# Four units routed ahead in the memory stage, the routing reordered, and expert tiles of 128 rows

## The chip, the cores and the metric

One core of a Trainium2 chip runs the whole program; the other cores are idle. The metric is the device time of one execution in microseconds (us). The core's engines are PE (TensorE: matmuls and transposes), DVE (VectorE), ACT (ScalarE), POOL (GpSimd) and SP (SyncE, which here only issues DMAs). Each has its own instruction queue; they meet through semaphores.

## The reference

The input x is 4 x 1024 tokens of 128 numbers, fp32. Four residual layers follow each other:

```python
x = x + attn(layernorm(x))     # softmax attention and a causal linear "memory" term, 16 heads
x = x + ffn(layernorm(x))
x = x + mamba(layernorm(x))    # selective scan, 256 inner channels, state 16
x = x + ffn(layernorm(x))

def ffn(x):                    # x: 4096 tokens x 128
    shared = (silu(x @ sw1) * (x @ sw2)) @ sw3           # 128 -> 256 -> 128
    probs = softmax(x @ rw + rb)                         # 8 experts
    w, idx = top_k(probs, 2); w = w / sum(w)
    routed = sum over the two chosen e of  w_e * ((silu(x @ ew1[e]) * (x @ ew2[e])) @ ew3[e])
    return shared + routed
```

The reference computes every expert for every token; the kernel computes for each token only the two chosen ones.

## The kernel before

**Stages in time.** Projection (0 to 87 us of the profiled span), softmax attention (to 618), the memory term (to 752), the first FFN's routing (to 841) and its experts (to 968), the scan (to 1545), the second FFN's routing (to 1641) and experts (to 1768), and a last sum of the rows.

**The memory stage** (`memory`, L934 on) walks over 32 blocks t of 128 tokens, eight for each of four batches. For each block PE makes masked products, which DVE masks in three parts and POOL in the fourth; then outputs, then a state of 128x128 that goes on to the next block. Four blocks are a half, which is also a unit of 512 tokens: when a half is done it is projected, x is added (`add_x`) and the result x1 is stored to DRAM by ACT (`store_x1`, two alternating tiles and semaphores). SP loads each batch ahead (`load_batch`). Into this loop the routing of the first two units of the next FFN is woven by hand, at given blocks: DVE's `mean_dve` (statistics of the layer norm), POOL's `rstd_pool`, DVE's `norm_dve`, PE's `turn_pe` (transposes), `logits_pe`, DVE's `choose_dve` and `settle_dve` (top 2), ACT's `tanh_act` (the gates), PE's `rank_pe` (ranks of the tokens within their experts by matmuls with a triangle), DVE's `place_dve` and `label_dve` (rows and token numbers), and POOL's `scatter`. These PE steps share the PSUM tile ps_p with `turn_ka` and `project_half`, so the waits of these are set by the order of the steps. SP loads the units' x back from DRAM at L1123 to L1129, after the third batch's load and the router's weights rw and rb (`load_choice`, L1409 and L1410).

**The routing** (`Router`, L1360 on, and `route`, L1576 on). A unit of 512 tokens gives 1024 pairs of token and expert; a scatter is an indirect DMA issued by POOL that writes 128 normalized rows, each with its token number and gate, to the row of `ex` in DRAM that its expert and rank give: eight scatters a unit, 64 for 4096 tokens. In `route`, `first` is the number of units that were routed ahead (2 in the first FFN, 0 in the second). The last of these is held: its eight scatters are issued in `route`. Each turn s also runs one unit of the shared FFN: `share_pe` and `silu_act`, `share_dve`, `back_pe` (L1628), `base_dve`, and a store by SP. When the last unit is placed, DVE makes two small tables: for each expert tile its expert (`name_experts`, L1831 to L1844) and its first row of `ex` (`name_rows`, L1853 to L1858), by wide operations over tiles x 8. Zero rows are stored behind each expert's rows (`pads`) so that a last tile reads valid rows.

**The experts** (`run_experts`, L1861 on). Each expert's rows are cut into tiles of ROWS = SUB x 128; with whole tiles per expert there are at most TOP * N / ROWS + 8. A loop runs over AHEAD tiles, unrolled, and jumps back. For each tile: SP reads the first row from the table into a register and loads the rows (AHEAD buffers); DVE reads the expert's number and copies the two weight matrices ew1 and ew2 to a fixed tile (L1933); PE transposes the rows (L1977), ACT evicts xT (L2007), PE makes ps_h (L1970), ACT the silu (L2002), DVE the product hid (L1940), PE makes ps_o (L1959) with ew3 at an address from a register that it loads at L1953, ACT evicts with the gate (L1995), POOL scatters 128 rows of results to `ey` (L2021). PE works on three tiles in one turn of its body, in this order:

```python
e = pe.value_load(at_expert[0:1, number_of(ti, tq)])   # L1953: tile q - 3
pe.wait_ge(hid_ready, now(s - 2))
...                                                    # ps_o, SUB x 2 matmuls, L1959
pe.wait_ge(xT_ready, now(s + 0))                       # tile q - 1
pe.wait_ge(w12_ready, now(s + 0))                      # L1967
...                                                    # ps_h, 4 matmuls, L1970
pe.wait_ge(loaded[q], now(i * 16 + 16))                # tile q
pe.wait_ge(xT_ready, now(s - 1))                       # L1975
...                                                    # SUB transposes, L1977
```

## Time and profile before

| | us |
|---|---|
| runs of the kernel before | 1784.13, 1785.74, 1794.47 |
| their median | 1785.74 |
| the profiled execution's own time | 1792.23 |
| its span, first to last instruction | 1790.5 |
| mean granted clock of PE | 0.859 |
| busy over the span: PE, DVE, POOL, ACT | 1362.6, 1266.3, 880.4, 855.2 |

The profile is of one execution. PE is the matmul array, PEld its weight loads (which overlap), PEq or PEldq the queue that reads PE's instructions; a share of busy time over the whole span is a mean over stages with different limits, so the stages are read one by one. A fp32 matmul stands in the rows as two instructions, a transpose as one. Matmuls are pipelined: the row's duration of one reaches into the next, and the distance of two starts is what one costs. The idle time before an instruction stands in brackets with what ended it ("issue" where nothing that the profile shows did).

### The profile page before, as it was taken

The page shows a single profiled execution, that of the slowest core. Times are in us where ns is not written, and L with a number is a line of the kernel's source. Part 1 is how long each engine was busy: PE and PEld are TensorE (multiplying, and loading weights), DVE is VectorE, ACT ScalarE, POOL GpSimd, SP SyncE. Part 2 cuts the span into 40 slices and gives each one's busy share as a digit, 9 for nine tenths or more (in the row PEclk, how much of TensorE's full clock was granted, in tenths as well). Part 3 has the DMA queues.
Part 4 walks back from the last instruction along what each step waited for, and adds up shares of the span by engine and source line. Part 5 has one row for each costly group of instructions (what it writes and reads, how often), then busy time and mean ns, then how long its engine had stood idle before and what let it go on. Part 6 is the DMA issues. An engine that isn't in the chain of part 4 may idle for free. (4 is left out here: it accounts for less than half of the span.)

```text
span 1790.5 us, 27815 instructions
## 1 busy us (share of the span) xinstructions
PE 1362.6 (76%) x8207; PEld 677.6 (38%) x8208; DVE 1266.3 (71%) x2981; ACT 855.2 (48%) x1215; POOL 880.4 (49%) x775
## 2 busy tenths in 40 slices
PE   3448999999999898785995777586676544584993
PEld 1213333333333265553994232131221200353992
DVE  3666899999989267674333279998998999573343
ACT  3403666666666734221553668467476332121551
POOL 3400212121211454675665248869869666475662
PEclk9655999999999999997997888698788656797996
DMA  4821111111112232254333395976957863624336
GB/s 121 265 73 48 53 49 55 47 58 44 61 47 65 54 84 84 86 159 108 85 93 111 98 226 154 249 182 162 245 131 199 198 163 94 174 87 124 111 93 166
DMA packets 218312, 210.68 MB, mean 118 GB/s; under 512 B 49247, under 2 KB 188482, under 8 KB 215874
## 3 DMA queue, kind: packets, MB, share of 16 engines
q1 hardware_dynamic: 196174, 180.70, 37.7%
q0 software_dynamic: 9216, 19.02, 3.3%
q10 hardware_dynamic: 12800, 9.46, 1.8%
q8 instruction: 60, 0.98, 0.2%
q14 instruction: 62, 0.51, 0.1%
HBM read 145.27 MB, written 63.37 MB: 117 GB/s over the span
## 5 line engine op out<-in xcount | busy, mean ns | idle before, releaser
L804 ACT ACTIVATE attn_prob<-attn_ps_cols 128x1024 f32<-128x1024 f32 (+1 forms) x320 | 292.0, 940 | 219.7 <-PE attn_ps_cols L680 218.7
L2546 POOL TENSOR_TENSOR ssm_hc<-ssm_h,ssm_cb 128x1024 f32<-128x1024 f32 x128 | 300.5, 2355 | 136.1 <-DVE ssm_h L2529 112.3
L2529 DVE TENSOR_TENSOR_SCAN ssm_h<-ssm_decay,ssm_ps_u 128x1024 f32<-128x1024 f32 x128 | 292.7, 2287 | 29.9 <-ACT ssm_decay L2517 12.6
L830 POOL TENSOR_SCALAR_AFFINE_SELECT attn_prob<-attn_prob 128x512 f32<-128x512 f32 x128 | 81.2, 635 | 415.7 <-ACT attn_prob L804 415.7
L712 DVE CUSTOM_DVE_ANT_0 attn_ps_rows<-attn_ps_rows,const_mask_rows 128x384 f32<-128x384 f32 (+3 forms) x512 | 236.1, 522 | 39.5 <-PE attn_ps_rows L647 37.3
L647 PE MATMUL attn_ps_rows<-attn_ks,attn_qs 72*128 72x512 bf16 (+3 forms) x768 | 228.8, 351 | 44.3 <-DMA attn_qs<-parts_dram 31.0
L2517 ACT ACTIVATE ssm_decay<-ssm_wide,ssm_aneg 128x1024 f32<-128x1024 f32 x128 | 146.1, 1146 | 173.5 <-DVE ssm_h L2529 97.1
L2480 PE MATMUL ssm_ps_u<-ssm_stack,ssm_spread 96*128 96x512 bf16 x256 | 99.1, 479 | 154.0 <-DVE ssm_h L2529 147.4
L680 PE MATMUL attn_ps_cols<-attn_qs,attn_ks 75*128 75x512 bf16 (+3 forms) x768 | 194.3, 333 | 4.6 <-DMA attn_qs<-attn_nrows 3.9
L699 PE MATMUL attn_ps_o<-attn_prob,attn_vw 128*32 128x512 f32 (+3 forms) x1536 | 166.6, 506 | 0.3 <-POOL attn_prob L830 0.3
L717 DVE TENSOR_REDUCE attn_nm<-attn_ps_rows 128x1 f32<-128x512 f32 x256 | 157.8, 682 | 7.8 <-PE attn_ps_rows L647 7.7
L2524 DVE TENSOR_TENSOR ssm_ps_u<-ssm_ps_u,ssm_bb 128x1024 f32<-128x1024 f32 x128 | 154.8, 1209 | 8.7 <-PE ssm_ps_u L2480 8.7
L647 PEld LDWEIGHTS attn_ps_rows<-attn_ks,attn_qs 72*128 72x128 bf16 x768 | 71.4, 100 | 180.4 <-DVE attn_nm L712 65.0
L2480 PEld LDWEIGHTS ssm_ps_u<-ssm_stack,ssm_spread 96*128 96x128 bf16 x256 | 17.3, 103 | 252.9 <-DVE ssm_h L2529 202.7
L680 PEld LDWEIGHTS attn_ps_cols<-attn_qs,attn_ks 75*128 75x128 bf16 x768 | 69.9, 100 | 87.8 <-ACT attn_prob L804 35.5
L2021 POOL DMA_INDIRECT ey_dram<-ffn1e_out,ffn1e_x x80 | 76.6, 957 | 50.9 <-ACT ffn1e_out L1995 38.3
L2021 POOL DMA_INDIRECT ey_dram<-ffn2e_out,ffn2e_x x80 | 76.6, 957 | 50.1 <-ACT ffn2e_out L1995 37.5
L2496 PE MATMUL ssm_ps_y<-ssm_hc,ssm_gather 128*32 128x512 f32 x512 | 83.4, 782 | 7.6 <-POOL ssm_hc L2546 7.6
L1970 PE MATMUL ffn1e_ps_h<-ffn1e_xT,ffn1e_w 128*128 128x256 f32 x320 | 77.6, 386 | 0.9 <-ACT ffn1e_xT L2007 0.9
L1970 PE MATMUL ffn2e_ps_h<-ffn2e_xT,ffn2e_w 128*128 128x256 f32 x320 | 77.1, 384 | 0.9 <-ACT ffn2e_xT L2007 0.9
L1096 DVE TENSOR_TENSOR mem_am<-mem_ps_a,const_strict 128x512 f32<-128x512 f32 x96 | 60.3, 684 | 20.6 <-PE mem_ps_a L1014 20.5
L1940 DVE TENSOR_TENSOR ffn1e_hid<-ffn1e_act,ffn1e_ps_h 128x512 f32<-128x512 f32 x40 | 27.5, 688 | 66.0 <-PE ffn1e_ps_h L1970 66.0
(361 smaller groups left out, 2438.6 us busy)
## 6 DMA issues: line engine op xcount, KB each, us to landing
ssm_wide<-delta_dram SPq DMA_DIRECT2D x128, 512.0 KB, 6.4
attn_ks<-parts_dram SPq DMA_DIRECT2D x48, 192.0 KB
attn_qs<-parts_dram SPq DMA_DIRECT2D x48, 192.0 KB
parts_dram<-proj_parts SPq DMA_DIRECT2D x8, 768.0 KB, 3.8
ffn1e_x<-ex_dram SPq DMA_DIRECT2D x40, 130.0 KB, 2.3
ffn2e_x<-ex_dram SPq DMA_DIRECT2D x40, 130.0 KB, 2.3
split_dram<-ssm_parts SPq DMA_DIRECT2D x6, 768.0 KB, 4.3
ssm_stack<-split_dram SPq DMA_DIRECT2D x18, 256.0 KB, 4.5
```

Of the source, the lines that this page charges most:

```text
L647: done = nc.tensor.matmul(out[:, x * w:(x + 1) * w], qs[k][0:KROWS, h, blk * P:(blk + 1) * P], ks[k][0:KROWS, h, half * QW:half * QW + w], ...
L680: done = nc.tensor.matmul(out[:, x, 0:w], ks[k][:, h, j * P:(j + 1) * P], qs[k][:, h, at:at + w], start=True, stop=True, skip_group_check= ...
L699: done = nc.tensor.matmul(ps_o[32 * h:32 * h + 32, at - ch * QW:at - ch * QW + w], vw[k % 2][:, j, h, :], prob[u % RING][:, h, 0:w], start ...
L712: done = nc.vector.tensor_tensor_reduce(scores, scores, c["mask_rows"][:, QW - w:], -1.0, -MINUS, ALU.add, ALU.min, into[:, h, at:at + 1])
L717: nc.vector.tensor_reduce(to, ps_rows[bank][:, 0:len(heads) * w].rearrange("p (h w) -> p h w", w=w), AX.X, ALU.max, negate=True).then_inc( ...
L804: nc.scalar.activation(prob[u % RING][:, heads[0]:heads[-1] + 1, 0:w], ps_cols[s % 2][:].rearrange("p b (x q) -> p (b x) q", x=len(heads) ...
L1970: done = nc.tensor.matmul(ps_h[n][z][:, h, :], w12[z][:, n * HIDDEN + h * P:n * HIDDEN + (h + 1) * P], xT[z][:], start=True, stop=True)
L2021: nc.gpsimd.indirect_dma_start(dram["ey"], bass.IndirectOffsetOnAxis(ap=x[q][:, j, TOKEN:TOKEN + 1].bitcast(I32), axis=0), out[q % OUTS][: ...
L2517: nc.scalar.activation(decay[t % DECAY_RING][:], wide[t % WIDE_RING][:], ACT.Exp, scale=aneg[:, at:at + 1]).then_inc(decay_ready, 1)
L2524: nc.vector.tensor_tensor(ps_u[t % 2][:], ps_u[t % 2][:], bb[b % 2][:], ALU.mult).then_inc(dbx_done, 1)
L2529: nc.vector.tensor_tensor_scan(h[t % H_RING][:], decay[t % DECAY_RING][:], ps_u[t % 2][:], 0.0, ALU.mult, ALU.add).then_inc(scan_done, 1)
L2546: nc.gpsimd.tensor_tensor(hc[:, t % HC_RING, :], h[t % H_RING][:], cb[b % 2][:], ALU.mult).then_inc(hc_done, 1)
```

## The change

- **Memory stage.** Four units instead of two are routed ahead, on one regular plan: unit u has its statistics at block 9 + 4u, norm and rstd at 10 + 4u, transposes at 11 + 4u, logits and choice at 12 + 4u, settle at 13 + 4u, the gates at 14 + 4u, rank, place and label at 15 + 4u. `set_up_dve` goes from block 9 to 8. From block 16 to 27 POOL issues two scatters per block (24, units 0 to 2; before, 8 in blocks 24 to 27). x1 is stored one block earlier. SP loads units 0 and 1 back after the third batch's load, units 2 and 3 after the fourth's.
- **Routing.** `first` is 4 in the first FFN: 8 held scatters and 32, where it was 8 and 48. While units 4 to 6 are routed, two units of the shared FFN run per turn. Within a turn the shared part stands between the logits and the rank; in the turn of the last unit the table of experts is made before the shared part, and the table of rows after it. xT has a tile for each unit.
- **Experts.** Tiles of 128 rows: 72 where it was 40, twelve in a turn of the loop where it was eight, six output tiles where it was eight. The zero rows are half as many.

```diff
@@ memory
-TURNED_BEHIND = {5: 1, 7: 2}
+STATS_AT, NORM_AT, TURN_AT, LOGITS_AT, SETTLE_AT, TANH_AT, RANK_AT, SEND_AT = 9, 10, 11, 12, 13, 14, 15, 16
+def unit_at(t, first):
+    u, rest = divmod(t - first, HALF)
+    return u if rest == 0 and 0 <= u < AHEAD_UNITS else None
@@ memory: sync
                         load_choice(sp, r, a)
-                        for u in range(AHEAD_UNITS):
-                            sp.wait_ge(x1_stored[u], 16)
+                    if i >= 2:
+                        for u in (2 * i - 4, 2 * i - 3):
+                            sp.wait_ge(x1_stored[u % 2], u // 2 * 16 + 16)
...
@@ memory: vector
-                    if t == 9:
+                    if t == 8:
                         set_up_dve(nc, r, c, dve)
-                    if t in (12, 15):
-                        mean_dve(nc, r, dve, (t - 12) // 3)
-                    if t in (13, 16):
-                        norm_dve(nc, r, dve, (t - 13) // 3)
+                    if unit_at(t, STATS_AT) is not None:
+                        mean_dve(nc, r, dve, unit_at(t, STATS_AT))
+                    if unit_at(t, NORM_AT) is not None:
+                        norm_dve(nc, r, dve, unit_at(t, NORM_AT))
...
@@ memory: scalar
-                    if t % HALF == 0 and half >= 2:
-                        store_x1(half - 2)
+                    if t % HALF == HALF - 1 and half >= 1:
+                        store_x1(half - 1)
@@ memory: gpsimd
-                    if t in (12, 15):
-                        rstd_pool(nc, r, pool, (t - 12) // 3)
-                    if 24 <= t < 28:
+                    if unit_at(t, NORM_AT) is not None:
+                        rstd_pool(nc, r, pool, unit_at(t, NORM_AT))
+                    if SEND_AT <= t < SEND_AT + (AHEAD_UNITS - 1) * HALF:
                         for j in range(2):
-                            scatter(nc, r, dram, pool, 0, (t - 24) * 2 + j)
+                            scatter(nc, r, dram, pool, (t - SEND_AT) // HALF, (t - SEND_AT) % HALF * 2 + j)
@@ sizes
-SUB = 2
+SUB = 1
-AHEAD = 8
-OUTS = 8
+AHEAD = 12
+OUTS = 6
+SENT = 4
-AHEAD_UNITS, AHEAD_ENDS = 2, [1, 2, 3, 5, 7, UNITS_IN]
-EXPERT_STRIDES = [AHEAD, 16, SUB * 16]
+AHEAD_UNITS, AHEAD_ENDS = 4, [1, 2, 3, 4, 5, 7, UNITS_IN]
+EXPERT_STRIDES = [AHEAD, 16]
@@ route
+        def shared_in(s):
+            if not first:
+                return [s - 1] if s else []
+            done = 2 * (s - first)
+            return [u for u in (done, done + 1) if u < s] if s < UNITS_IN - 1 else [s - 1]
@@ route: tensor
-                for u in range(first - 1):
-                    share_pe(u, 0)
-                    share_pe(u, 1)
-                for s in range(first, UNITS_IN + 2):
+                for s in range(first, UNITS_IN + 1):
+                    shares = shared_in(s)
                     if s < UNITS_IN:
                         turn_pe(nc, r, c, s)
-                    if s >= 2:
-                        back_pe(s - 2)
+                    if shares:
+                        pe.wait_ge(s_loaded, 3 * 16)
+                        share_pe(shares[0], 0)
                     if s < UNITS_IN:
                         logits_pe(nc, r, s)
-                    if 1 <= s <= UNITS_IN:
-                        share_pe(s - 1, 0)
-                        share_pe(s - 1, 1)
+                    if shares:
+                        if shares[0]:
+                            back_pe(shares[0] - 1)
+                        share_pe(shares[0], 1)
                     if s < UNITS_IN:
                         rank_pe(nc, r, s)
+                    if len(shares) > 1:
+                        share_pe(shares[1], 0)
+                        back_pe(shares[0])
+                        share_pe(shares[1], 1)
+                back_pe(UNITS_IN - 1)
@@ route: vector (the order within a turn)
+                    if s < UNITS_IN:
+                        choose_dve(nc, r, dve, s)
+                        settle_dve(nc, r, dve, s)
+                    if s + 1 < UNITS_IN:
+                        norm_dve(nc, r, dve, s + 1)
+                    if shares:
+                        share_dve(dve, shares[0], 0)
+                        if shares[0]:
+                            base_dve(dve, shares[0] - 1)
+                        share_dve(dve, shares[0], 1)
+                    if s < UNITS_IN:
+                        place_dve(nc, r, dve, s)
+                        label_dve(nc, r, dve, s)
+                    if s == UNITS_IN - 1:
...
                         steps = name_experts(nc, dve, t, r.count, step_dve, tabled)
...
+                name_rows(nc, dve, t, step_dve, tabled, steps)
+                base_dve(dve, UNITS_IN - 1)
```

## Rows read from the trace of the kernel before

**Rows 1.** Busy time by stretch: engine, busy us (instructions); then PE clock, DMA share, GB/s.

```profile
618.00:752.40 134.40, 121.49 (x1587) 79.10 (x1587) 89.28 (x219) 47.70 (x83) 73.28 (x70) 0.94 0.30 84
752.40:841.00 88.60, 58.69 (x294) 38.72 (x294) 53.81 (x283) 18.35 (x35) 65.11 (x66) 0.85 0.53 149
841.00:968.00 127.00, 116.86 (x720) 104.97 (x720) 44.71 (x81) 64.19 (x160) 77.02 (x82) 0.96 0.31 84
...
1641.00:1768.00 127.00, 116.32 (x720) 104.67 (x720) 45.07 (x80) 64.19 (x160) 76.58 (x80) 0.96 0.36 101
```

**Rows 2.** Timeline of PE, experts, first FFN: start, us, line, operation, tiles, count.

```profile
868.99 1.89 PE L1970 MATMUL ffn1e_ps_h<-ffn1e_xT,ffn1e_w 128*128 128x256 f32 x8
870.72 0.38 PE L1977 MATMUL ffn1e_ps_x<-const_ident,ffn1e_x 128*128 128x128 f32 x2
870.94 1.06 PE L1959 MATMUL ffn1e_ps_o<-ffn_w,ffn1e_hid 128*128 x8
871.83 1.89 PE L1970 MATMUL ffn1e_ps_h<-ffn1e_xT,ffn1e_w 128*128 128x256 f32 x8
```

**Rows 3.** PE's queue in one tile: line, operation, ns min/median/max, first and last start.

```profile
L1953 PEldq TENSOR_LOAD <-ffn_at_expert x2: 303/304/305, 866.3 to 869.1; - x2
L1959 PEldq SEQ_ASSERT  x4: 18/18/18, 867.0 to 867.7; - x4
L1967 PEldq EVENT_SEMAPHORE  x1: 51/51/51, 867.9 to 867.9; - x1
L1975 PEldq EVENT_SEMAPHORE  x1: 51/51/51, 868.8 to 868.8; - x1
```

**Rows 4.** Timeline of ACT, the same tile: the eviction of xT.

```profile
868.38 0.39 ACT L2007 ACTIVATE ffn1e_xT<-ffn1e_ps_x 128x256 f32<-128x256 f32 x1 [0.56 <-PE ffn1e_ps_x L1977]
```

**Rows 5.** PE's queue, last two loads of an expert number in the loop's end.

```profile
L1953 PEldq TENSOR_LOAD <-ffn_at_expert x2: 301/302/303, 956.8 to 958.4; - x2
```

**Rows 6.** Groups by line and shape, experts: busy us, mean ns | idle before.

```profile
L2021 POOL DMA_INDIRECT ey_dram<-ffn1e_out,ffn1e_x x80 | 76.6, 957 | 50.9 <-ACT ffn1e_out L1995 38.3 <-issue 12.3 <-DMA ey_dram<-ffn1e_out,ffn1e_x 0.3
L1933 DVE COPY ffn1e_w<-ffn_w 128x512 f32 x40 | 17.1, 429 | 21.1 <-issue 19.0
```

**Rows 7.** Timeline of SP's DMA issues, memory stage.

```profile
655.84 0.35 SPq L979 DMA_DIRECT2D early_qaT<-fT_dram  x1
...
661.64 2.19 SPq L1409 DMA_DIRECT2D ahead_rw<-in_L_ffn_rw_dram  x1
...
664.48 10.35 SPq L1127 DMA_DIRECT2D ahead_x<-x_dram  x2
```

**Rows 8.** The tile ahead_x in 655 to 680 us: from DMA issue to landing.

```profile
DMA to landing us min/median/max: 2.8/3.7/4.6
```

**Rows 9.** Timeline of DVE, memory stage: the end of set_up_dve.

```profile
662.65 0.17 DVE L1573 TENSOR_SCALAR ahead_count<-ahead_number 128x8 f32<-128x8 f32 x1
```

**Rows 10.** Waits in 630 to 750 us: engine, line, releaser: us in total, times, longest.

```profile
PE mem_ps_y L1037 <- POOL mem_am L1285: 4.4, 2, 2.3
```

**Rows 11.** Timeline of POOL, memory stage: the mask around two scatters.

```profile
727.19 1.28 POOL L1285 TENSOR_TENSOR mem_am<-mem_raw,const_strict 128x512 f32<-128x512 f32 x1
...
730.93 1.27 POOL L1285 TENSOR_TENSOR mem_am<-mem_raw,const_strict 128x512 f32<-128x512 f32 x1
```

**Rows 12.** Timeline of POOL, first routing: its last scatter.

```profile
837.36 0.95 POOL L1549 DMA_INDIRECT ex_dram<-ffn1r_xn,ffn1r_pos  x1 [0.31 <-issue]
```

**Rows 13.** Timeline of PE, first routing: one unit to the next.

```profile
801.72 2.05 PE L1628 MATMUL ffn1r_ps_o<-ffn1r_sw,ffn1r_hid 128*128 128x128 f32 x16 [0.24 <-DVE ffn1r_hid L1608]
...
804.42 3.68 PE L1621 MATMUL ffn1r_ps_h<-ahead_xnT,ffn1r_sw 128*128 128x512 f32 x8
...
808.93 2.05 PE L1628 MATMUL ffn1r_ps_o<-ffn1r_sw,ffn1r_hid 128*128 128x128 f32 x16 [0.23 <-DVE ffn1r_hid L1608]
```

**Rows 14.** Timeline of DVE, first routing: one wide operation on the tables.

```profile
819.93 0.48 DVE L1840 TENSOR_TENSOR ffn_mine<-ffn_begun,ffn_over 1x320 f32<-1x320 f32 x1
```

**Rows 15.** Timeline of POOL, second routing: its first scatter.

```profile
1553.61 1.11 POOL L1549 DMA_INDIRECT ex_dram<-ffn2r_xn,ffn2r_pos  x1 [4.51 <-DVE ffn2r_xn L1436]
```

More of the change, by code:

```diff
@@ L1137, in _ @@
                         products(t + 1)
+                    u = unit_at(t, RANK_AT)
+                    if u is not None:
+                        if u == 0:
+                            pe.wait_ge(r.set_up, 3)
+                        pe.wait_ge(x1_ready, u + 3)
+                        rank_pe(nc, r, u)
                     outputs(t)
@@ L1730, in _ @@
-                    if first < s < UNITS_IN:
-                        choose_dve(nc, r, dve, s)
-                        settle_dve(nc, r, dve, s)
-                    if s == first + 2:
-                        for u in range(first + 5, UNITS_IN):
+                    if len(shares) > 1:
+                        share_dve(dve, shares[1], 0)
+                        base_dve(dve, shares[0])
+                        share_dve(dve, shares[1], 1)
+                    if s <= first + 1:
+                        for u in range(first + 3 + 2 * (s - first), min(first + 5 + 3 * (s - first), UNITS_IN)):
@@ L1735, in _ @@
                             mean_dve(nc, r, dve, u)
[L1736 to L1738 removed]
+                name_rows(nc, dve, t, step_dve, tabled, steps)
+                base_dve(dve, UNITS_IN - 1)
             @block.scalar
             def _(act):
[L1742 to L1744 removed]
                 for s in range(first, UNITS_IN + 1):
+                    shares = shared_in(s)
@@ L2013, in _ @@
                 m.wipe(pool)
-                turns = Turns(pool, stage + "_pool", sorted(set(EXPERT_STRIDES + [SUB * AHEAD])), first=1)
+                turns = Turns(pool, stage + "_pool", EXPERT_STRIDES, first=1)
                 def body(i, at, q, on):
@@ L2083, in routing_scratch @@
     for stage in stages:
-        dram[stage + "r_sent"] = [m.sem(f"{stage}_sent{k}") for k in range(DEEP)]
+        dram[stage + "r_sent"] = [m.sem(f"{stage}_sent{k}") for k in range(SENT)]
         dram[stage + "e_sent"] = [m.sem(f"{stage}_out{q}") for q in range(AHEAD)]
```

137 lines of the change are left out of this document (49 added, 88 removed).

## The prediction

> **What bounds the kernel now.** I read the busy time by stretch first, because the change touches four stretches with different limits [rows 1]. In each expert stage PE is busy 116.9 of 127 us, and no other engine is near it. In the memory stage PE is busy 121.5 of 134.4 us. In the first routing no engine is full: POOL leads with 65.1 of 88.6 us. Attention and the scan keep their code, so they keep their time.
>
> Next I read PE's timeline in the expert stage. One 256-row tile repeats every 2.84 us (868.99 to 871.83) [rows 2]. The spacing of starts prices it: eight ps_h instructions from 868.99 to 870.72, 0.216 each; two transposes, 0.22; eight ps_o instructions from 870.94, 0.89, so 0.111 each. The array is never idle, so today it sets the pace.
>
> Third came PE's queue, the part that reads instructions and fills registers. It loads the expert's number (L1953) at 866.3 and at 869.1, works out the weight addresses, and reaches the wait of L1967 at 867.9 [rows 3]. That is 1.6 us of scalar work per tile, whatever the tile's height. Then it stands until 868.8 (L1975). ACT's eviction of xT runs from 868.38 for 0.39 us, to 868.77 [rows 4]: the queue goes on when xT is there. So the 0.9 us from L1967 to L1975 is mostly waiting, and the 1.6 us is work, hidden today under 2.84 us of array. At the stage's end, with no new tile to transpose, two loads still stand 1.6 us apart (956.8, 958.4) [rows 5].
>
> **The change, part 1: experts, 72 tiles of 128 rows.** Array work per tile: ps_h 8 x 0.111, one transpose 0.11, ps_o 4 x 0.111, together 1.44 us. 72 x 1.44 = 103.7 against 40 x 2.84 = 113.6: on the array alone, less. The queue's work per tile shrinks only by the steps of the second half, two of the four assertions of L1959 (four lie between 867.0 and 867.7) [rows 3], about 0.2. What remains is 1.6 - 0.2 = 1.4 from load to L1967; from L1975 to the next load 0.3 (868.8 to 869.1); and the wait's own 0.05 plus the reading of eight ps_h instructions, which the rows do not separate from the waiting. I take 0.15 for both, because the queue reads the ps_o instructions within its 1.6 as well. Sum 1.85, and with the jump back once in twelve tiles about 1.9 us. The chain transpose, xT, ps_h of one tile does not exceed it: 0.89 of the ps_h ahead in the array, 0.27 for the transpose, 0.39 at most for the eviction, 1.55. Nor do others: POOL's scatter takes 0.957 and a pause of 0.30, 1.26 a tile; DVE copies weights for 0.43 as before, since a tile's weights don't shrink [rows 6].
>
> Bounds for this period: below, 1.44, if the array hides all the queue's work; above, 1.4 + 0.3 + 0.9 = 2.6, if nothing between L1967 and L1975 is waiting. I take 1.9, nearer the lower end, because the queue resumed within 0.1 us of the eviction's end.
>
> Per FFN: 127.0 today is 113.6 and 13.4 of fill and drain. The drain is three tiles deep, so it shortens by 3 x (2.84 - p). After: 72p + 13.4 - 3 x (2.84 - p) = 75p + 4.9. Against 127.0 that is 75p - 122.1; at p = 1.9, +20.4. Both FFNs: **+41**. At the bounds -28 and +146.
>
> This rests on the scalar load's 0.303 us [rows 3]. The Trainium skill ("DMA: Bandwidth & Descriptors", Latency and other measured facts) gives a floor of about 600 ns for a `tensor_load`, and says that the compiler unrolls fourfold to amortize it, a rule against small tiles. This trace shows half that price; by the page's, an estimate of p = 2.2 and of +86 for this term.
>
> **Part 2: memory stage.** DVE's statistics for unit 0 move to block 9, behind set_up_dve, which ends at 662.8 [rows 9]. The x they need is loaded by SP behind the batch load that starts at 655.84 and behind rw and rb; it is issued at 664.48 [rows 7] and lands up to 4.6 later [rows 8]: 669.1. DVE would stand 6.3 us, and its products' masks and state, for which PE waits, are queued behind. Unit 2, at block 17, meets the same order behind the next batch load without rw and rb (2.8 us less): I take 4.5. Removed: PE's waits on POOL's mask, which stands behind rstd, 4.4 us in two waits [rows 10]. Added on PE: turn, logits and rank of two more units, each 7.21 - 5.4 = 1.8 (part 3), +3.6. Added on POOL: 16 scatters; a block with two of them takes POOL 3.74 us (727.19 to 730.93) [rows 11], against a block of 134.4 / 32 = 4.2, so POOL is close to the pace in twelve blocks instead of four: 0 to 8, I take 4. Where one stall covers another I take off 2. Sum 6.3 + 4.5 - 4.4 + 3.6 + 4 - 2 = **+12**, bounds +2 (x is in time) and +18.
>
> **Part 3: first routing.** Sixteen scatters fewer. The last one starts at 837.36, and one costs 0.95 + 0.31 = 1.26 [rows 12]: POOL's chain shortens by 20.2. PE becomes the tighter one for a while. A unit takes 7.21 us on PE (801.72 to 808.93); the shared FFN's part is 3.5 of L1621 and 1.9 of L1628, 5.4, the durations less the overlap with what follows [rows 13]. Two shares per routed unit make 10.8 + 1.8 = 12.6, over 8 x 1.26 = 10.1 of POOL. So the gain is not whole: three such rounds lose 2.5 each over POOL's pace, but the first begins before POOL's scatters of its unit, and I count about 3 lost. Behind them the tables: a wide operation takes 0.48 us on 320 elements [rows 14]; on 576 I scale it to 0.75. Eight of them, +2.2, and they now stand ahead of the last unit's share and sum, which must still run and be stored. 20.2 - 3 - 2.2 = **-15**; bounds -21 and -12. The halved zeros and the longer tables that POOL writes among its scatters I set against each other.
>
> **Part 4: second routing.** All 64 scatters stay, one behind another from 1553.61 on; the first waits 4.51 us for unit 0 [rows 15]. The new order lets unit 0 be placed without norm of later units ahead of it: **-1**, bounds -3 and +2.
>
> **Sum.** 41 + 12 - 15 - 1 = +37 on the profiled execution: its own time is 1792.23 (span 1790.5), which is 6.5 over the median 1785.74 of the runs. I add the difference to the median: 1785.7 + 37 = 1823, stated as 1822.
>
> **The rivals.** (B, the other side) The queue's work is hidden: the array holds enough instructions that the scalar work of one tile runs under the matmuls of another, and the chain of 1.55 us sets p = 1.55 or less. For it: the array is never idle today [rows 2]. Against it: the queue stands at L1967 until xT is there [rows 3, 4], so it can't run ahead into the next tile. At p = 1.5, 75 x 1.5 - 122.1 = -9.6 for each FFN; -19 + 12 - 15 - 1 = -23, so 1763. It decides from p below 1.655, where the whole sum is nought; a time under 1768 needs p = 1.54. The Trainium skill ("Advanced Engine Details and Errata", Sequencer Loop) says that other engine instructions can be read and queued while a control instruction executes. If that held across tiles, p would be 1.5; the rows that show the queue released by xT speak against it.
>
> (C) x is not late in the memory stage, because x1 is stored one block earlier and SP is there in time. Against it: SP, not the store, was late (rw, rb and the batch load ahead) [rows 7]. Then +2 for that stage: 41 + 2 - 15 - 1 = +27, 1813.
>
> (D) PE's clock falls in the expert stages. PE would stand idle 0.46 of each 1.9 us, where today it never stands [rows 2]; the granted clock is 0.96 in the expert stage, and 0.85 in the first routing, where PE stands between its units [rows 1]. If a sixth of the tiles ran at the lower level, 1.2 instead of 2.4 GHz, they would take 2 x 1.44 = 2.88: 24 tiles x 0.98 = +24, so 1846.
>
> (E) In between: p between 1.54 and 1.77, since the reading of ps_h may cost nothing and the address work may be shorter in other code. Then the time lies from 1768 to 1803, no change that counts.
>
> **How the numbers follow.** Forecast (p near 1.9, x late) 0.43, D 0.17, C 0.11, E 0.19, B 0.10. A measurement of this kernel can tell about 1%, 18 us, from no change: faster is under 1768, slower over 1803.6. Faster 0.10 (B), same 0.19 (E), slower 0.71. The range 1790 to 1850 takes in the forecast, C, D and the upper half of E; below it lie B and E's lower half, above it a period nearer 2.6, a price that only the upper bound has.
>
> **What would show it right or wrong.** In the expert stage of after: distance of successive TENSOR_LOADs of PE's queue about 1.9 us, PE busy about 105 of 147 us, and L1967's wait at once followed by L1975, no 0.9 us between. If the loads stand 1.5 apart, part 1 is wrong and the kernel may be faster. In the memory stage: SP's load of the first x issued after DVE's set_up, statistics idle about 6 us on a DMA, the stage near 146 us. In the first routing: 40 scatters, end of stage 73 us after its start. The granted clock of the expert stage tells D. Most of all the forecast falls if the queue's 1.6 us is not work but pace kept by something behind it.

## The result

The changed kernel took 1828.5 us (median of 4 runs, 1826.2 to 1830.5) against 1785.5 for the kernel before: 1.021 times, with a 95% interval of 1.0185 to 1.0234. It is slower by 43 us, 2.1%, with an interval clear of no change and on both sides of 2%; 1822 was forecast, with 1790 to 1850 as the range.

The busy time by stretch of the changed kernel (us; PE, PEld, DVE, ACT, POOL, each with its instructions; then granted clock, DMA share, GB/s):

```profile
618.30:772.00 153.70, 128.61 (x1621) 83.45 (x1621) 108.29 (x299) 50.56 (x89) 91.60 (x88) 0.91 0.30 84
772.00:845.50 73.50, 53.70 (x260) 35.26 (x260) 46.79 (x204) 15.82 (x29) 47.48 (x49) 0.88 0.49 143
845.50:987.30 141.80, 133.00 (x936) 114.31 (x936) 69.63 (x144) 74.14 (x216) 69.04 (x72) 0.97 0.25 68
...
1660.60:1804.80 144.20, 133.43 (x936) 114.63 (x936) 68.63 (x144) 74.14 (x216) 68.91 (x72) 0.96 0.30 81
```

From the first instruction of each stage to the first of the next, in the two profiled executions:

| stage | before | after | difference | forecast |
|---|---|---|---|---|
| up to the memory stage | 618.7 | 618.9 | +0.2 | 0 |
| memory | 133.8 | 153.1 | +19.3 | +12 |
| first routing | 88.6 | 73.5 | -15.1 | -15 |
| first experts | 126.4 | 141.8 | +15.4 | +20.4 |
| scan | 568.6 | 568.4 | -0.2 | 0 |
| second routing | 104.7 | 104.9 | +0.2 | -1 |
| second experts | 125.9 | 144.2 | +18.3 | +20.4 |
| join | 23.7 | 23.9 | +0.2 | 0 |

So the routing gave back what it was meant to give, and the two expert stages and the memory stage took 53 us.

**The experts.** PE's timeline in the first expert stage of the changed kernel:

```profile
880.64 1.06 PE L1975 MATMUL ffn1e_ps_h<-ffn1e_xT,ffn1e_w 128*128 128x128 f32 x8
881.53 0.27 PE L1982 MATMUL ffn1e_ps_x<-const_ident,ffn1e_x 128*128 128x128 f32 x1
881.66 0.94 PE L1964 MATMUL ffn1e_ps_o<-ffn_w,ffn1e_hid 128*128 x4
882.44 1.06 PE L1975 MATMUL ffn1e_ps_h<-ffn1e_xT,ffn1e_w 128*128 128x128 f32 x8
```

A tile repeats every 1.80 us (880.64 to 882.44), where 2.84 stood for twice the rows [rows 2]. The four ps_o instructions last from 881.66 to 882.44, 0.78, though they need 4 x 0.111: the array stands within them. PE's queue in the same stretch (line, operation, ns min/median/max, first and last start):

```profile
L1958 PEldq TENSOR_LOAD <-ffn_at_expert x2: 300/304/307, 880.8 to 882.6; - x2
L1972 PEldq EVENT_SEMAPHORE  x3: 51/51/51, 880.4 to 884.1; - x3
L1980 PEldq EVENT_SEMAPHORE  x3: 51/51/51, 880.6 to 884.3; - x3
```

The load still takes 0.30. The queue reaches the wait for the weights (L1972; before, L1967) at 880.4 and goes through the next one (L1980; before, L1975) at 880.6. Before, 0.9 us stood between those two [rows 3]; now nothing waits there. In 62 of the stage's 64 tiles that have both events in the trace, 0.25 us or less lie between them. The queue is not released late: it is itself late.

The second expert stage grew by 3 us more than the first. Only there SP loads `ffn_base` behind the first twelve tiles' rows (L1923, 12.0 us from issue to landing), and the rows of the next tile are issued behind it; PE stands for them:

```profile
1673.38 0.82 SPq L1923 DMA_DIRECT2D ffn_base<-base_dram  x1
1685.69 0.32 PE L1982 MATMUL ffn2e_ps_x<-const_ident,ffn2e_x 128*128 128x128 f32 x1 [1.11 <-DMA ffn2e_x<-ex_dram]
```

Around it two tiles took 4.02 and 2.78 us instead of 1.80. That the load of `ffn_base` makes these rows late is read from the order of the queue; no run takes it away.

**The memory stage.** Its waits in the changed kernel (engine, line, releaser: us in total, times, longest):

```profile
DVE ahead_stats L1419 <- DMA ahead_x<-x_dram: 7.8, 2, 6.2
PE mem_ps_p L1493 <- DVE ahead_count L1472: 7.6, 2, 4.2
...
PE mem_ps_y L1043 <- POOL mem_am L1285: 2.3, 3, 1.1
```

DVE stood 7.8 us on the x that SP loads back, 6.2 of it for unit 0, whose load stands in SP's queue behind a batch load and the router's weights. The wait of PE on POOL's mask fell from 4.4 [rows 10] to 2.3. PE has a wait that was not there: the transposes of a unit stand behind the counts of the unit before (L1493), 7.6 us in two waits. DVE's norm in its timeline, with POOL's beside it:

```profile
672.71 1.11 DVE L1434 TENSOR_SCALAR ahead_xn<-ahead_x,ahead_mv,ahead_rstd 128x128 f32<-128x128 f32 x4
...
690.20 3.29 DVE L1434 TENSOR_SCALAR ahead_xn<-ahead_x,ahead_mv,ahead_rstd 128x128 f32<-128x128 f32 x4
...
730.49 4.84 DVE L1434 TENSOR_SCALAR ahead_xn<-ahead_x,ahead_mv,ahead_rstd 128x128 f32<-128x128 f32 x4
```

```profile
689.30 2.35 POOL L1278 TENSOR_TENSOR mem_xb<-early_x,mem_bias 128x1024 f32<-128x1024 f32 x1
691.61 1.28 POOL L1285 TENSOR_TENSOR mem_am<-mem_raw,const_strict 128x512 f32<-128x512 f32 x1
...
730.89 1.27 POOL L1285 TENSOR_TENSOR mem_am<-mem_raw,const_strict 128x512 f32<-128x512 f32 x1
732.12 2.35 POOL L1278 TENSOR_TENSOR mem_xb<-mem_x_in,mem_bias 128x1024 f32<-128x1024 f32 x1
```

Four norm instructions take 1.11 us at 672.71, but 3.29 and 4.84 at 690.20 and 730.49, where POOL adds the bias to x (L1278) and masks (L1285); those at 709.98 take 2.55, beside a scatter and a mask. The last group ends at 735.33, 0.9 us after POOL's addition; its first instruction alone took 4.07 us. The groups by line of the changed kernel (us in all, mean ns; the norm of the memory stage), and the same of the kernel before:

```profile
L1434 DVE TENSOR_SCALAR ahead_xn<-ahead_x,ahead_mv,ahead_rstd 128x128 f32<-128x128 f32 x16 | 11.8, 797 | 0.0
```

```profile
L1436 DVE TENSOR_SCALAR ahead_xn<-ahead_x,ahead_mv,ahead_rstd 128x128 f32<-128x128 f32 x8 | 2.2, 341 | 0.0
```

An instruction that took 341 ns takes 797 in the mean. Counted over all of DVE's operations of the stage, as time beyond the shortest of the same kind (where it is over 0.06 us), this standing is 10.4 us in the changed kernel, in seven instructions, each beside POOL's mask or addition. In the kernel before it is 1.2 us in three; the largest stood beside the mask of [rows 11], where one of two instructions took 0.83 us and the other 0.15:

```profile
727.67 0.91 DVE L1455 TENSOR_TENSOR ahead_gap<-ahead_top 128x4 f32<-128x4 f32 x2
```

**The first routing.** POOL and PE of the changed kernel, and a wide operation of the table of experts:

```profile
819.06 0.95 POOL L1544 DMA_INDIRECT ex_dram<-ffn1r_xn,ffn1r_pos  x1 [2.39 <-DVE ffn1r_xn L1486]
...
840.22 0.96 POOL L1544 DMA_INDIRECT ex_dram<-ffn1r_xn,ffn1r_pos  x1 [0.30 <-issue]
```

```profile
809.02 0.60 PE L1493 MATMUL ffn1r_ps_x<-const_ident,ffn1r_xn 128*128 128x128 f32 x4
...
821.30 0.60 PE L1493 MATMUL ffn1r_ps_x<-const_ident,ffn1r_xn 128*128 128x128 f32 x4
```

```profile
832.88 0.74 DVE L1845 TENSOR_TENSOR ffn_mine<-ffn_begun,ffn_over 1x576 f32<-1x576 f32 x1
```

A round of two shared units and one routed unit takes PE 12.28 us (809.02 to 821.30), POOL waits for the place of the next unit (2.39 at 819.06), and the last scatter ends at 841.2, 69 us after the stage began; before, it ended 86 us after [rows 12].

### The profile page after: what moved, and what is told of

Read it like the earlier page. It is cut to its first block and busy times, and to the rows that moved or that the text cites. A ratio compares the mean times of both kernels' runs of the same rounds, so it can differ in the third digit from the quotient of the medians.

```text
span 1828.7 us, 30675 instructions
## 1 busy us (share of the span) xinstructions
PE 1395.8 (76%) x8639; PEld 697.1 (38%) x8640; DVE 1327.5 (73%) x3110; ACT 875.7 (48%) x1327; POOL 867.3 (47%) x760
## 5 line engine op out<-in xcount | busy, mean ns | idle before, releaser
L2529 DVE TENSOR_TENSOR ssm_ps_u<-ssm_ps_u,ssm_bb 128x1024 f32<-128x1024 f32 x128 | 154.9, 1210 | 10.3 <-PE ssm_ps_u L2485 10.2
L647 PEld LDWEIGHTS attn_ps_rows<-attn_ks,attn_qs 72*128 72x128 bf16 x768 | 71.5, 100 | 180.6 <-DVE attn_nm L712 64.9
L2026 POOL DMA_INDIRECT ey_dram<-ffn2e_out,ffn2e_x x72 | 68.9, 957 | 76.1 <-ACT ffn2e_out L2000 72.0
L2026 POOL DMA_INDIRECT ey_dram<-ffn1e_out,ffn1e_x x72 | 69.0, 959 | 75.3 <-ACT ffn1e_out L2000 72.5
L1975 PE MATMUL ffn2e_ps_h<-ffn2e_xT,ffn2e_w 128*128 128x128 f32 x576 | 79.1, 282 | 0.7 <-ACT ffn2e_xT L2012 0.7
L1975 PE MATMUL ffn1e_ps_h<-ffn1e_xT,ffn1e_w 128*128 128x128 f32 x576 | 78.7, 281 | 0.7 <-ACT ffn1e_xT L2012 0.7
L1938 DVE COPY ffn2e_w<-ffn_w 128x512 f32 x72 | 38.3, 532 | 55.8 <-issue 32.5
L1544 POOL DMA_INDIRECT ex_dram<-ffn2r_xn,ffn2r_pos x64 | 62.6, 979 | 23.4 <-issue 17.7
```

Of the source, the lines that this page charges most:

```text
L647: done = nc.tensor.matmul(out[:, x * w:(x + 1) * w], qs[k][0:KROWS, h, blk * P:(blk + 1) * P], ks[k][0:KROWS, h, half * QW:half * QW + w], ...
L1975: done = nc.tensor.matmul(ps_h[n][z][:, h, :], w12[z][:, n * HIDDEN + h * P:n * HIDDEN + (h + 1) * P], xT[z][:], start=True, stop=True)
L2026: nc.gpsimd.indirect_dma_start(dram["ey"], bass.IndirectOffsetOnAxis(ap=x[q][:, j, TOKEN:TOKEN + 1].bitcast(I32), axis=0), out[q % OUTS][: ...
L2529: nc.vector.tensor_tensor(ps_u[t % 2][:], ps_u[t % 2][:], bb[b % 2][:], ALU.mult).then_inc(dbx_done, 1)
```

## The experiments

Stages of every run, from its own trace (us; the tile is the middle value of the distance between the ps_h of successive tiles in the first expert stage). Runs given below without a ratio are single executions. The kernel before had medians of 1789 to 1794 us beside the experiments and 1785.5 beside the changed kernel, so single runs are compared by their stages rather than by the whole time:

| run | memory | routing 1 | experts 1 | routing 2 | experts 2 | tile |
|---|---|---|---|---|---|---|
| before | 133.8 | 88.6 | 126.4 | 104.7 | 125.9 | 2.84 |
| changed | 153.1 | 73.5 | 141.8 | 104.9 | 144.2 | 1.80 |
| t128_only | 133.6 | 88.7 | 141.0 | 104.9 | 142.2 | 1.80 |
| t256_rest | 153.0 | 74.9 | 126.7 | 104.8 | 126.1 | 2.84 |
| fixed_w3 | 153.1 | 73.4 | 128.6 | 104.7 | 128.5 | 1.63 |
| two_loads | 154.1 | 71.3 | 141.3 | 104.7 | 142.0 | 1.80 |
| turned_first | 153.4 | 73.4 | 140.9 | 104.8 | 143.3 | 1.81 |
| turned_first_fixed_w3 | 152.8 | 73.4 | 116.4 | 105.1 | 122.2 | 1.45 |
| two_loads_used | 153.0 | 73.4 | 169.5 | 105.1 | 168.7 | 2.24 |
| x_direct | 146.3 | 73.4 | 141.8 | 105.4 | 142.3 | 1.80 |
| bias_later | 159.2 | 73.0 | 141.0 | 105.1 | 142.1 | 1.80 |
| both_256 | 147.1 | 75.1 | 126.2 | 104.8 | 127.2 | 2.84 |
| all_128 | 147.6 | 71.5 | 116.1 | 105.2 | 122.6 | 1.45 |
| all_128_bias1 | 146.7 | 71.9 | 115.8 | 105.0 | 120.2 | 1.45 |

**Which half of the change costs what.** The tiles alone in the kernel before:

```diff
-SUB = 2
+SUB = 1
-AHEAD = 8
-OUTS = 8
+AHEAD = 12
+OUTS = 6
```

> The kernel before with only the expert tiles changed (72 of 128 rows, 12 in a turn, 6 output tiles; the scatters of the routing count on four semaphores instead of eight, as in the changed kernel, which leaves semaphores for the 12). Theory A (PE's queue sets 1.84 us per tile): the two expert stages grow as in the changed kernel, by 15 and 18 us, and the wider tables add 0 to 4 us, so 1820 us (1814 to 1826). Rival (the expert stages are slow only behind the new routing, or most of the 43 us comes from the memory stage): at most half of that, under 1805.

Measured: 1823.6 us, 1.0165 of the kernel before (1.0126 to 1.0203), about 30 us. The expert stages grew by 14.6 and 16.3, the routing by 0.1: theory A, and the wider tables add at most 0.2 us to a routing.

The other half, tiles of 256 rows back in the changed kernel:

```diff
-SUB = 1
+SUB = 2
-AHEAD = 12
-OUTS = 6
+AHEAD = 8
+OUTS = 8
```

> The changed kernel with 40 expert tiles of 256 rows again; memory stage and routing stay as changed. Theory A: what is left is the memory stage (+19 us) and the first routing (-15), and the narrower tables give back up to 2 us each: 1788 us (1783 to 1794), its expert stages at 2.84 us per tile again. Rival (the two parts need each other, for instance because the routing's gain comes from the smaller tiles and their fewer zero rows): the first routing longer than 80 us, or the total over 1797.

Measured: 1799.0 us beside 1792.4 for the kernel before in the same runs, 1.0032 (1.0013 to 1.0051). The time itself lies above the expected range and above the rival's 1797. But both were reckoned from a kernel before of 1785.5: the difference expected was -2.5 to +8.5 us, and 6.5 was measured; the routing is far from the rival's 80 us.

The expert stage is as before, the routing keeps 13.7 us of its gain, and the memory stage keeps its 19. The two ratios multiply to 1.0197, close to the whole change's 1.021: the halves do not need each other.

**Is it PE's queue?** PE reads no number; all tiles take the third weights of expert 0:

```diff
-                        e = pe.value_load(at_expert[0:1, number_of(ti, tq)])
...
-                                flat[:, ds(e + (2 * HIDDEN + h * D), D)],
+                                flat[:, 2 * HIDDEN + h * D:2 * HIDDEN + (h + 1) * D],
```

> The changed kernel, in which PE doesn't read the expert's number: ps_o is made with the third weights of expert 0 for every tile, so the routed part of the result is that of another network; all else, the copies of the first two weights too, is as it was. Theory A (the scalar work of PE's queue sets the pace): the distance of two tiles falls from 1.80 us to the next bound, the chain transpose, xT, ps_h of 1.55 us or the array's 1.44, so 144 tiles give back 36 to 52 us: 1777 to 1793. Rival (DVE's own load and copy of weights, 0.42 + 0.43 + 0.58 + 0.37 us a tile, or the chain through ACT sets the pace, and the queue only follows): 1.75 us or more per tile, over 1820.

Measured: 1802.4 us, 26 less (29 in the two expert stages), 1.63 us a tile. That is between the two expectations: the queue did set the pace, but the next bound lies higher than the text had it. PE and ACT of this run:

```profile
901.74 0.27 PE L1981 MATMUL ffn1e_ps_x<-const_ident,ffn1e_x 128*128 128x128 f32 x1
...
902.38 1.16 PE L1974 MATMUL ffn1e_ps_h<-ffn1e_xT,ffn1e_w 128*128 128x128 f32 x8
903.37 0.27 PE L1981 MATMUL ffn1e_ps_x<-const_ident,ffn1e_x 128*128 128x128 f32 x1
```

```profile
902.04 0.28 ACT L2011 ACTIVATE ffn1e_xT<-ffn1e_ps_x 128x128 f32<-128x128 f32 x1 [0.17 <-PE ffn1e_ps_x L1981]
```

Transpose at 901.74, xT from 902.04 to 902.32, ps_h at 902.38, and the next transpose, which stands behind those eight ps_h, at 903.37: a closed chain of 1.63. It was put at 1.55; the first of the eight ps_h, begun after the array stood, is followed by the next after 0.21 us and not 0.11. So even without a single scalar step, tiles of 128 rows in this order gain nothing: 128.6 and 128.5 us against 126.4 and 125.9.

The other way round, the reading twice:

```diff
                         e = pe.value_load(at_expert[0:1, number_of(ti, tq)])
+                        e2 = pe.value_load(at_expert[0:1, number_of(ti, tq)])
```

> The changed kernel, in which PE's queue reads the expert's number twice for each tile. Theory A: each tile takes the second load's 0.30 us longer, and up to 0.11 of register work with it: 144 x 0.30 to 0.41 = 43 to 59 us more, 1871 to 1888. Rival (the queue's work is hidden or only half exposed): less than 20 us more.

Measured: 1829.1 us. This run says nothing of the queue: its trace holds 72 loads in the first expert stage, one for each tile, so the second reading, whose value nobody used, did not come into the program that ran. It is in effect the changed kernel once more, and shows how far single runs differ: 154.1 us in the memory stage and 71.3 in the first routing, against 153.1 and 73.5. With each half of ps_o on its own reading:

```diff
-flat[:, ds(e + (2 * HIDDEN + h * D), D)]
+flat[:, ds((e2 if h else e) + (2 * HIDDEN + h * D), D)]
```

> The changed kernel, in which PE's queue reads the expert's number twice for each tile and uses one reading for each half of ps_o, so that neither can fall away. Theory A: 0.30 us and up to 0.11 of register work more per tile, 144 x 0.30 to 0.41 = 43 to 59 us more than the changed kernel. Rival (the queue's work is hidden): less than 15 us more.

Measured: 1882.1 us, 54 more; 144 loads in the stage, and 2.24 us a tile, 0.44 more. PE's timeline (idle time before and what ended it in brackets):

```profile
900.60 0.91 PE L1965 MATMUL ffn1e_ps_o<-ffn_w,ffn1e_hid 128*128 x4 [0.23 <-issue]
...
902.90 0.91 PE L1965 MATMUL ffn1e_ps_o<-ffn_w,ffn1e_hid 128*128 x4 [0.39 <-DVE ffn1e_hid L1945]
...
905.06 0.91 PE L1965 MATMUL ffn1e_ps_o<-ffn_w,ffn1e_hid 128*128 x4 [0.25 <-issue]
```

PE stands ahead of ps_o. In two of these three the profile names no releaser but "issue", its queue; in one DVE's product ended last. The pace is the queue's all the same: its loads of successive tiles start at 901.53 and 903.82, 2.28 us apart, with gaps under 0.1 us between its instructions.

Then the chain alone. The transpose of the next tile is issued ahead of ps_h, and ACT evicts xT ahead of the silu (PE's part of the edit):

```diff
+                    if on[0]:                       # tile q: transposes
+                        ...
                     if on[1]:                       # tile q - 1: ps_h
                         ...
-                    if on[0]:
-                        ...
```

> The changed kernel with PE's transpose of tile q issued before ps_h of tile q - 1 instead of behind it, and ACT's eviction of xT before the silu: the chain transpose, xT, ps_h is taken out of the way (1.63 us a tile where PE reads no expert's number). Theory A (the queue's scalar work sets the pace, 1.80): no change, 1.78 to 1.84 us a tile, 1824 to 1832 us. Rival (the chain sets the pace and the queue only follows it): 1.65 us or less a tile, 20 us less or more.

Measured: 1832.0 us, 1.81 a tile: no change.

```profile
900.98 1.06 PE L1982 MATMUL ffn1e_ps_h<-ffn1e_xT,ffn1e_w 128*128 128x128 f32 x8
...
902.78 1.06 PE L1982 MATMUL ffn1e_ps_h<-ffn1e_xT,ffn1e_w 128*128 128x128 f32 x8
```

The chain was not the pace of the changed kernel.

The same order, with the fixed weights of fixed_w3:

> The same order, and PE reads no expert's number: ps_o uses the third weights of expert 0 for every tile, so that the routed part of the result is that of another network. Theory A, with the chain as the bound that came next at 1.63 us: with both gone the array's 1.44 us is left, 1.44 to 1.52 a tile, so the two expert stages lose another 17 to 27 us against the run with the old order: 1775 to 1786 us. Rival (1.63 was DVE's copy of the weights or POOL's scatter, not the chain): still 1.60 or more, about 1800 us.

Measured: 1781.5 us, 1.45 a tile:

```profile
880.41 1.06 PE L1981 MATMUL ffn1e_ps_h<-ffn1e_xT,ffn1e_w 128*128 128x128 f32 x8
881.30 0.61 PE L1963 MATMUL ffn1e_ps_o<-ffn_w,ffn1e_hid 128*128 128x128 f32 x4
881.75 0.27 PE L1971 MATMUL ffn1e_ps_x<-const_ident,ffn1e_x 128*128 128x128 f32 x1
881.86 1.06 PE L1981 MATMUL ffn1e_ps_h<-ffn1e_xT,ffn1e_w 128*128 128x128 f32 x8
```

880.41 to 881.86 is 1.45, and no instruction has idle time before it: this is the array's 1.44. So there are three bounds one above another in the changed expert stage: PE's queue at 1.80, the chain at 1.63, the array at 1.44.

**The memory stage.** The units' x stays on the core: `add_x` writes halves 0 to 3 into the router's own tiles, and SP's loads fall away:

```diff
+        def x1_of(half):
+            return r.x[half] if half < AHEAD_UNITS else x1[half % 2]
...
-            nc.vector.tensor_tensor(x1[half % 2][:], ps_p[:], ...
+            nc.vector.tensor_tensor(x1_of(half)[:], ps_p[:], ...
```

> The changed kernel, in which the four units' x stays where the memory stage makes it: add_x writes units 0 to 3 into the router's tiles, and SP's four loads fall away. Theory M1 (x comes late, DVE stands 6.2 and 1.6 us on it with PE's masks behind): both waits go, the memory stage falls from 153 us by 5 to 8. Rival M2 (the stage is long because DVE's operations on SBUF stand while POOL works, and the waits for x only cover part of that, or are off the path): less than 3 us.

Measured: the memory stage takes 146.3 us, 6.8 less, and DVE's wait on x is gone; the whole took 1817.4. M1 holds for a third of the 19 us. Its 16 norm instructions still take 790 ns each, so what is left is not x.

POOL's addition of the bias away from the norm (the edit moves it from the last block of the batch before to a batch's fifth block):

```diff
-                    if t % BLK == 7 and t // BLK + 1 < B:
-                        add_bias(t // BLK + 1)
+                    if t % BLK == 4 and t >= BLK:
+                        add_bias(t // BLK)
```

> The changed kernel, in which POOL adds the bias to x (L1278, 2.35 us, reading and writing SBUF) three blocks before the end of a batch's last half no longer, but in the batch's fifth block, away from DVE's norm of units 1 and 3. Theory M2 (DVE's norm from SBUF to SBUF stands while POOL reads SBUF): the four norm instructions of units 1 and 3 fall from 3.29 and 4.84 us together to under 2 each, and the memory stage falls from 153 us by 2 to 6. Rival (they are slow for the scatters' sake, or by themselves): norms as before, stage within 1 us.

Measured: the stage takes 159.2 us, 6 more, where 2 to 6 less was expected. The norm did fall (516 ns, from 797; unit 1 to 1.11 us, unit 3 only to 2.54), but another DVE operation took its place, and DVE's wait for x grew from 7.8 to 10.3. DVE's groups, and one of these operations with POOL beside it:

```profile
L1474 DVE TENSOR_TENSOR ahead_rows<-ahead_pick,ahead_row 128x32 f32<-128x32 f32 x8 | 8.7, 1129 | 0.0
L1434 DVE TENSOR_SCALAR ahead_xn<-ahead_x,ahead_mv,ahead_rstd 128x128 f32<-128x128 f32 x16 | 7.3, 516 | 0.0
```

```profile
712.74 3.38 DVE L1474 TENSOR_TENSOR ahead_rows<-ahead_pick,ahead_row 128x32 f32<-128x32 f32 x2
712.39 1.27 POOL L1285 TENSOR_TENSOR mem_am<-mem_raw,const_strict 128x512 f32<-128x512 f32 x1
713.62 2.35 POOL L1278 TENSOR_TENSOR mem_xb<-early_x,mem_bias 128x1024 f32<-128x1024 f32 x1
```

The two products of place (L1474, 128 x 32, both operands in SBUF) take 3.38 us from 712.74 to 716.12; POOL's mask and addition run from 712.39 to 715.97. In the changed kernel eight of them took 2.7 us, here 8.7. That such operations stand while POOL masks and adds is shown; its remedy by this move failed. The rival, that the scatters slow them, is weak: beside a scatter alone, in the two routings of the kernel before, a norm instruction took 333 to 546 ns.

**A version from these.** Tiles of 256 rows, x kept, the bias as in the last run:

> The changed kernel with 256-row tiles, x kept on the core and the bias added elsewhere. If the three causes add up: the run with 256-row tiles alone stood 1.0032 of the kernel before (+6 us); 7 from x and 2 to 6 from the bias come off: 0.996 to 1.001 of the kernel before. Rival (the gains in the memory stage cover each other): as the run with 256-row tiles, 1.003.

Measured: 0.9983 of the kernel before (0.9970 to 0.9995), as expected, but without the gain expected from the bias: its memory stage takes 147.1 us, and with x kept alone it took 146.3.

Tiles of 128 rows, the transpose first, x kept, the bias as in the last run, and the third weights copied by DVE with the others, so that PE needs no register:

```diff
-                        nc.vector.tensor_copy(w12[q % 2][:], flat[:, ds(e, 2 * HIDDEN)])
+                        nc.vector.tensor_copy(w12[q % 4][:], flat[:, ds(e, EW)])
...
-                                flat[:, ds(e + (2 * HIDDEN + h * D), D)],
+                                w12[(q - 3) % 4][:, 2 * HIDDEN + h * D:2 * HIDDEN + (h + 1) * D],
```

> The changed kernel with 128-row tiles, the transpose issued first, x kept and the bias moved, and the third weights copied by DVE with the first two (768 columns instead of 512, four buffers), so that PE reads no expert's number. By theory A PE's queue is out of the way; DVE takes 0.42 (product), 0.43 (its own reading) and 0.64 to 0.85 (copy) a tile, 1.5 to 1.7: expert stages of 118 to 130 us each, the whole 0.990 to 1.002 of the kernel before. Rival (DVE's copy stands while POOL writes its scatters, or the longer copy becomes the pace): over 1.8 us a tile, 1.01 and more.

Measured: 1772.4 us, 0.9876 of the kernel before (0.9855 to 0.9897): 1.2% faster than the kernel before, and better than the 0.990 to 1.002 expected: DVE's copy did not become the pace. Two changes meet in it, the reading taken from PE and the order of the transpose; turned_first and turned_first_fixed_w3 show them apart. PE in its first expert stage, and DVE's copy (us in all, mean ns):

```profile
899.84 1.06 PE L1982 MATMUL ffn1e_ps_h<-ffn1e_xT,ffn1e_w 128*128 128x128 f32 x8
...
901.29 1.06 PE L1982 MATMUL ffn1e_ps_h<-ffn1e_xT,ffn1e_w 128*128 128x128 f32 x8
L1939 DVE COPY ffn1e_w<-ffn_w 128x768 f32 x72 | 41.5, 576 | 37.4 <-issue 20.5 <-PE ffn1e_ps_o L1964 16.6
```

1.45 us a tile with the right weights. DVE's copy of 768 columns takes 576 ns, where 640 to 850 were expected, and its work is hidden under the array's. The second expert stage takes 6.5 us more than the first; PE stands 4.2 us there for the rows behind `ffn_base`.

The last run moves the bias once more, to a batch's second block (`t % BLK == 1`):

> As all_128, but POOL adds the bias in a batch's second block (blocks 9, 17, 25), where DVE meanwhile does choose, max and index, and masks from PSUM, and no norm and no place. Theory M2 (DVE's operations with all their operands in SBUF stand while POOL's vector operations read SBUF): the norm stays near 7.3 us in all (16 instructions), the two products of place (L1475, eight instructions) fall from 8.8 us to 2.7 or less, and the memory stage falls from 147.6 to 139 to 144 us; the whole 0.982 to 0.987 of the kernel before. Rival (the bias's place has nothing to do with it, what is left is PE's added work): the stage stays at 146 to 149.

Measured: 1774.9 us, 0.9905 (0.9871 to 0.9938), and 146.7 us for the memory stage instead of 147.6. The expectation missed, and the stage lies in the rival's 146 to 149. DVE's groups of this run, and one of the slow operations with POOL beside it:

```profile
L1475 DVE TENSOR_TENSOR ahead_rows<-ahead_pick,ahead_row 128x32 f32<-128x32 f32 x8 | 4.3, 576 | 0.0
L1463 DVE TENSOR_TENSOR ahead_chosen<-ahead_pick 128x32 bf16<-128x32 f32 x4 | 4.2, 1044 | 0.1
...
L1569 DVE TENSOR_SCALAR ahead_region<-ahead_number 128x8 f32<-128x8 f32 x1 | 2.3, 2331 | 0.0
```

```profile
691.08 2.39 POOL L1278 TENSOR_TENSOR mem_xb<-early_x,mem_bias 128x1024 f32<-128x1024 f32 x1
...
695.95 1.27 POOL L1285 TENSOR_TENSOR mem_am<-mem_raw,const_strict 128x512 f32<-128x512 f32 x1
695.45 1.83 DVE L1463 TENSOR_TENSOR ahead_chosen<-ahead_pick 128x32 bf16<-128x32 f32 x1
```

The products of place fell to 4.3, not to 2.7, and now L1463 takes 4.2 us (0.8 in the changed kernel) and one instruction of L1569 takes 2.3. Only that last one stands behind the addition: the additions at 691.08 and 731.52 lengthened nothing of DVE. L1463, and what is left of the norm and the products, stand beside POOL's mask (L1285), which no run moved.

## Why the prediction was right, and where it was not

**The experts, right.** +33.7 measured, +41 forecast. The period was put at 1.9: it is 1.80, and 2.3 once in twelve tiles where the loop jumps back, 1.85 in the mean of a turn. Both experiments on the load moved the time as the queue's theory says, by -0.17 and +0.44 a tile. The unknown of the step, how much of the 0.9 us between L1967 and L1975 was waiting, is settled: nearly all of it. My 0.15 for reading the ps_h there was measured at 0.13 (880.43 to 880.56 in the queue's events), and the work from the load to L1972 came out at 1.43, where 1.4 was taken; the rest, from L1980 to the next load, at 0.24 and not 0.3. One sign of the prediction did not show: PE was to be busy about 105 of 147 us, and the rows have 133.0 of 141.8. The rows count the array as busy where it stands within ps_o: four of them have 0.94 us here and 0.61 in turned_first_fixed_w3. The Trainium skill ("DMA: Bandwidth & Descriptors", Latency and other measured facts) has about 600 ns as the floor of such a load; the changed kernel's rows have 300 to 307, and one load more cost 0.44 with the register work around it.

**Rival B, wrong for a second reason.** It wanted 1.55 or less from a chain that is 1.63: ps_h takes 0.99 there and not 0.89 before the next transpose, since the first of the eight takes 0.21. At 1.63 the whole change would still have been no gain (fixed_w3, 1802.4). The Trainium skill ("Advanced Engine Details and Errata", Sequencer Loop) has the sequencer go on reading while a control instruction runs; no run here shows PE's queue going ahead of its own register work, and two_loads_used shows the array waiting for it.

**The memory stage, right in its sign, mis-sized.** +19.3 against +12, beyond the bound of +18. That the whole came as near as it did is in part luck: the experts were 7 us under their forecast, this stage 7 over. The first wait for x was 6.2 where 6.3 was worked out; the second 1.6 and not 4.5 (by my own rows 3.5, 6.3 less 2.8): DVE came to unit 0 6.7 us after SP began the batch load ahead of its x (655.80), as worked out, but to unit 2 11.1 us after the next one (692.52), since it was late for other reasons by then. Together the two waits are worth 6.8. The wait on POOL's mask fell by 2.1, not 4.4.

The sum lacked a whole term: DVE's operations on SBUF standing while POOL masks and adds (M2). By groups it is 16 x (797 - 341) ns = 7.3 us for the norm, at the 341 ns a norm took in the memory stage before, and some 3 us for the products of place and for the small sums of L1426 (2.7 and 2.1 us in all). How much of these 10 us lengthens the stage is not shown. And PE's term was too small: its busy time grew by 7.1 us, not 3.6, of which the routing's own matmuls are 5.8 by groups. The granted clock of the stage fell from 0.94 [rows 1] to 0.91; the products of the later batches (mem_ps_a) took 701 ns in the mean, 645 before.

I counted POOL's sixteen scatters as POOL's own time only (+4) and not what more work of POOL and DVE side by side does to DVE. Both norms of before ran while POOL was idle, so their rows did not show it; the operation at 727.67, shown above, did. In the first routing of before the first eight norm instructions had a mean of 502 ns, most of it beside other operations of POOL (iota, memset, scatters). The second thing not worked out is PE's new wait behind DVE's counts (7.6 us): the order puts the transposes of a unit right behind the place of the unit before, in the same block, so that whatever delays DVE there delays PE. That it follows from the standing of DVE is argued, not shown.

How the 12 us that remain without the waits for x divide between this standing of DVE and the added work of PE stays open. In the four runs with x kept, the standing counted as above is 10.7 (x_direct), 12.2 (all_128_bias1), 14.4 (both_256) and 14.5 us (all_128), and the stage takes 146.3, 146.7, 147.1 and 147.6. These differences are no larger than the spread of the seven runs that share the changed kernel's memory stage (152.8 to 154.1), so almost 4 us more of standing lengthened the stage by little if at all; that speaks against the standing as the main part. No run takes it away altogether, since the mask stayed on POOL in all of them.

**The first routing, right.** -15.1 against -15. PE's round was 12.28 where 12.6 was worked out; a wide operation on 576 elements took 0.74, as scaled [rows 14]. **The second routing:** +0.2 against -1, within its bounds.

**Rival C** (x is not late) is refuted by the 6.2 us, and its price of +2 by x_direct, where x is in time and the stage is still 12.5 us longer than before. **Rival D** (the clock falls): 0.97 and 0.96 in the expert stages, against 0.96 and 0.96 before. It did not happen there.

## What to carry to other kernels

A smaller tile divides the array's work but not the scalar work, the latency of the chain, nor the copy of the weights that each tile needs (the chain here went to 1.63 us, the array's part to 1.44); before halving a tile, add up what the engine's own queue does per tile and the shortest closed loop through the engines, and compare each with the new period of the array. Take an address that depends on data out of the busiest engine's queue and give the reading to an engine with time to spare: here that, with one reordering, turned a loss of 34 us in the expert stages into a gain of 14 (238.7 us for both, against 252.3). When work of two engines is woven together, look at what else each does at that moment, since operations that are short alone can stand behind one another; and before moving one, see from the trace which of them it stands behind, and whether the stage waits for it.

## What the runs showed of the hardware

DVE's scaling, adding and multiplying operations (tensor_scalar, tensor_tensor) with all operands in SBUF stand while POOL's mask (128 x 512) or addition (128 x 1024) runs: a norm of 128 x 128 took 0.34 us alone and up to 4.07 beside both, and two products of 128 x 32 ended 0.15 us after POOL's addition of 2.35. The masks that DVE makes from PSUM did not change (682 ns after, 684 before), and DVE's search for the maximum, whose operands are in SBUF too, kept its 0.15 and 0.16 us beside the addition at 731.52 (all_128_bias1). The Trainium skill ("SBUF — State Buffer", Who interferes with whom) states this: VectorE and GpSimd share a pair of ports under an exclusive lock, taken by `tensor_scalar` in a two-port mode and, against GpSimd's reads, by `tensor_tensor` with two inputs in SBUF. The rows with the mask and the addition agree, though no run shows in which mode the norm ran; the prediction had not weighed it. Not every operation of POOL holds DVE for its whole length: in the second routing of the kernel before, four norm instructions took 334 ns each beside POOL's rstd.

```profile
1575.41 2.33 POOL L1557 TENSOR_TENSOR ffn2r_rstd<-ffn2r_veps,ffn2r_power 128x12 f32<-128x12 f32 x1
1575.59 1.10 DVE L1436 TENSOR_SCALAR ffn2r_xn<-ffn2r_x,ffn2r_mv,ffn2r_rstd 128x128 f32<-128x128 f32 x4
```

One more reading of a number into a register cost PE's queue 0.30 us and 0.14 of register work around it (2.24 us a tile against 1.80), and PE's array stands for it where the queue is late.
